# Router logits of the first batch as eight more columns of the first expert's down products

## The chip, the cores and the metric

The kernel runs on one core of one Trainium2 chip. A core has TensorE (PE, with its weight loads as PEld), VectorE (DVE), ScalarE (ACT), GpSimd (POOL), and SyncE (SP), which issues transfers. Each engine works through its own queue in order and waits on semaphores that others raise. The metric is the device time of one execution in microseconds (us), as the median of several runs.

## The reference

Two layers over x of 2 x 1024 tokens by 256. The part that matters here lies in the first layer, between attention and a mixture of experts. The input of the router is the output of an expert MLP that is picked once per batch:

```python
expert = jnp.argmax(opcode_onehot, axis=-1)
up = jnp.einsum('bsd,bhd->bsh', x, wu) + bu[:, None, :]
gate = jnp.einsum('bsd,bhd->bsh', x, wg) + bg[:, None, :]
hidden = jax.nn.silu(up) * gate
out = jnp.einsum('bsh,bdh->bsd', hidden, wd) + bd[:, None, :]
...
x = hidden_states.reshape(N, d)          # out of the MLP above
logits = x @ Wg.T                        # 8 experts
top_v, top_i = jax.lax.top_k(logits, K)  # K = 2
pos = jnp.cumsum(onehot, axis=0) - 1     # a token's place with its expert
keep = pos_f < cap                       # cap = 640
exp_batches = jnp.zeros((E, cap, d), x.dtype).at[flat_e, pos_safe].set(x[tok], mode='drop')
```

Eight experts with GELU work on these batches, and their outputs are added with the gates. Attention stands ahead of this; a second layer (three MLPs, a scan, adapters and a feed-forward part) stands behind it.

## The kernel before

All products are fp32 values split in a high and a low part, and three products stand for one: high by high, low by high, high by low (`products`, L1093, whose three matmuls are L1095 to L1097). The 2048 tokens are four chunks of 512, `c` = 0 to 3; chunks 0 and 1 are batch 0, chunks 2 and 3 batch 1. A chunk has four tiles of 128 tokens.

The order on every engine is written out by hand in `plan()`: it appends units to one list per engine, and each program below walks its list. A unit waits by `ready(...)` for the units that it reads, and a unit on PE also for the one that held its PSUM bank before. The banks go round in rings: `work` has banks 0 to 2, `down` 3 to 5, `turn2` bank 6.

For chunk c, `up_units` puts eight units on PE: `up(c, i, part)` for i = 0 to 3, each six products of 128x512. For each i, ACT takes `silu` and `hid_hi` (L1494, L1500) and DVE `prod0` and `hid_lo` (L1789, L1793). `down(c, t)` is one tile of 128 tokens by 256 features, twelve products, and DVE's `xrow` (L1802) adds the bias of the down weights and so frees the bank; SP writes the rows to memory, from where they are gathered later by expert. The down bias comes by two small gathers that POOL issues in `phase0` (L2131) behind that of the second batch's expert weights (L2129).

The logits don't use the rows. `wg(b)` forms the router's weights through the down weights (512 by 8) once per batch, `lgT(c)` multiplies the hidden values with their high and low parts as 16 stationary columns (L1223, L1224, eight products of 128x512), ACT's `lg_row` copies the result, and `lg(c)` adds the two parts and turns them (L1230). DVE then finds the largest (`first`) and the second (`second`, `m16`, `first_row`), PE counts (`cnt`), DVE works out places (`pos`, `place`, `digits`) and `at` (L1858 to L1860), from which PE's `inv` (L1247) sums up the list of tokens by slot. Its last one releases the gathers.

The first expert's weights of batch 1 are split in six pieces, ACT's `w0_hi` (L1485) and POOL's `w0_lo_pool` (L2140). Every `up` of chunks 2 and 3 waits for the last of POOL's pieces:

```python
pe.wait_ge(*ready("x1_lo", c))
pe.wait_ge(*ready("w0_lo_pool" if b else "w0_lo", b, PIECES0 - 1))
```

These pieces come from a second generator, `weights`, which is moved one step at each `yield` of `all_chunks`; where a yield stands in `all_chunks` therefore sets where a piece stands on ACT and POOL.

## Time and profile before

| what | value |
|---|---|
| median of 3 runs | 940.58 us (940.43 to 941.33) |
| profiled execution | 934.67 us |
| its span, first to last instruction | 933.4 us |
| instructions | 13194 |
| PE busy | 919.2 us, 98% |
| DVE busy | 530.1 us, 57% |
| ACT busy | 446.8 us, 48% |
| POOL busy | 269.1 us, 29% |
| granted TensorE clock, mean | 1.000 |
| of the chain that ended last, on PE | 88% |

All rows are of this one profiled execution. Matmuls are pipelined, so the length shown for one (0.39 us for 128x512) is longer than the distance from its start to the next one's start; a price on PE is read from starts. On the other engines the length of one and the start of the next tell what it costs its queue. A row's bracket tells how long the engine was idle ahead of it and who ended that. The mean of a group mixes what stands in it.

### The profile page before, as it was taken

The page shows a single profiled execution, that of the slowest core. Times are in us where ns is not written, and L with a number is a line of the kernel's source. Part 1 is how long each engine was busy: PE and PEld are TensorE (multiplying, and loading weights), DVE is VectorE, ACT ScalarE, POOL GpSimd, SP SyncE. Part 2 cuts the span into 40 slices and gives each one's busy share as a digit, 9 for nine tenths or more (in the row PEclk, how much of TensorE's full clock was granted, in tenths as well). Part 3 has the DMA queues.
Part 4 walks back from the last instruction along what each step waited for, and adds up shares of the span by engine and source line. Part 5 has one row for each costly group of instructions (what it writes and reads, how often), then busy time and mean ns, then how long its engine had stood idle before and what let it go on. Part 6 is the DMA issues. An engine that isn't in the chain of part 4 may idle for free.

```text
span 933.4 us, 13194 instructions
## 1 busy us (share of the span) xinstructions
PE 919.2 (98%) x4895; PEld 773.6 (83%) x4895; DVE 530.1 (57%) x972; ACT 446.8 (48%) x831; POOL 269.1 (29%) x243
## 2 busy tenths in 40 slices
PE   7999999999999999999999999999999999999998
PEld 4768878888799999998888888888888888888786
DVE  6754453586757766786565564334333335688544
ACT  3666565433355545674343353353342443345775
POOL 1533221220275765664410153042140230010000
PEclk9999999999999999999999999999999999999999
DMA  8030001202255443432503003003003012000011
GB/s 299 30 113 23 25 1 68 80 23 96 67 142 148 144 154 135 126 107 86 180 23 136 23 23 136 1 0 136 1 1 136 0 44 92 1 1 1 0 46 46
DMA packets 22193, 67.49 MB, mean 72 GB/s; under 512 B 4514, under 2 KB 11954, under 8 KB 19314
## 3 DMA queue, kind: packets, MB, share of 16 engines
q1 hardware_dynamic: 16546, 40.15, 11.8%
q0 software_dynamic: 5440, 26.50, 9.6%
q8 instruction: 40, 0.66, 0.3%
q14 instruction: 23, 0.19, 0.1%
q10 hardware_dynamic: 144, 0.00, 0.0%
HBM read 55.09 MB, written 9.45 MB: 69 GB/s over the span
## 4 chain that ended last, share of the span: by engine, by line
PE 88%; DVE 5%; ACT 2%; issue 2%; DMA 2%; POOL 1%; SPq 0%; ACTq 0%; DVEq 0%; POOLq 0%
PE banks L1095 19%; PE banks L1097 18%; PE banks L1096 18%; PE banks L1328 5%; PE banks L1330 5%; PE banks L1329 5%; PE banks L1187 3%; PE banks L1171 2%; PE banks L1380 2%; PE banks L1379 2%; PE banks L1178 1%; PE banks L1367 1%; PE banks L1366 1%; DMA weight_stage<-in_cond_w 1%; PE banks L1255 1%
## 5 line engine op out<-in xcount | busy, mean ns | idle before, releaser
L1095 PE MATMUL banks<-input_hi,mlp_hi 128*128 128x512 f32 x376 | 147.6, 392 | 0.0
L1097 PE MATMUL banks<-input_hi,mlp_lo 128*128 128x512 f32 x376 | 146.4, 389 | 0.0
L1096 PE MATMUL banks<-input_lo,mlp_hi 128*128 128x512 f32 x376 | 146.4, 389 | 0.0
L1590 ACT CAST hidden_hi<-hidden 128x512 fp32r<-128x512 f32 x96 | 59.6, 621 | 161.2 <-DVE hidden L1995 110.0
L2185 POOL TENSOR_TENSOR mlp_lo<-weight_stage,mlp_hi 128x768 fp32r<-128x768 f32 x32 | 59.0, 1845 | 172.4 <-ACT mlp_hi L1564 172.4
L2001 DVE TENSOR_TENSOR hidden_lo<-hidden,hidden_hi 128x512 fp32r<-128x512 f32 x96 | 66.4, 692 | 62.0 <-ACT hidden_hi L1590 61.6
L1995 DVE SCALAR_TENSOR_TENSOR hidden<-banks,L_expert_weight,gelu 128x512 f32<-128x512 f32 x64 | 48.0, 751 | 84.8 <-PE banks L1097 81.3
L1584 ACT ACTIVATE gelu<-banks 128x512 f32<-128x512 f32 x96 | 57.4, 598 | 63.8 <-PE banks L1097 63.6
L1097 PEld LDWEIGHTS banks<-input_hi,mlp_lo 128*128 128x128 f32 x376 | 70.6, 188 | 14.8
L1095 PEld LDWEIGHTS banks<-input_hi,mlp_hi 128*128 128x128 f32 x376 | 70.6, 188 | 14.3
L1096 PEld LDWEIGHTS banks<-input_lo,mlp_hi 128*128 128x128 f32 x376 | 70.6, 188 | 14.3
L1095 PE MATMUL banks<-expert_in_hi,ffn_w_hi 128*128 128x256 f32 (+1 forms) x256 | 80.0, 313 | 0.1
L1097 PE MATMUL banks<-expert_in_hi,ffn_w_lo 128*128 128x256 f32 (+1 forms) x256 | 78.8, 308 | 0.0
L1096 PE MATMUL banks<-expert_in_lo,ffn_w_hi 128*128 128x256 f32 (+1 forms) x256 | 78.8, 308 | 0.0
L1328 PE MATMUL banks<-hidden_hi,mlp_hi 128*128 128x512 f32 x192 | 75.1, 391 | 0.0
L1330 PE MATMUL banks<-hidden_hi,mlp_lo 128*128 128x512 f32 x192 | 74.8, 390 | 0.0
L1329 PE MATMUL banks<-hidden_lo,mlp_hi 128*128 128x512 f32 x192 | 74.7, 389 | 0.0
L2145 POOL TENSOR_TENSOR ffn_w_lo<-weight_stage,ffn_w_hi 128x512 fp32r<-128x512 f32 x42 | 54.4, 1297 | 32.8 <-ACT ffn_w_hi L1523 32.7
L1927 DVE TENSOR_TENSOR expert_hidden_lo<-hidden,expert_hidden_hi 128x256 fp32r<-128x256 f32 (+1 forms) x64 | 46.4, 725 | 25.9 <-ACT expert_hidden_hi L1542 25.2
L2157 POOL DMA_INDIRECT gathered<-routed_input,token_of_slot x40 | 39.4, 984 | 72.2 <-DMA routed_input<-x_rows 56.0
L1997 DVE TENSOR_TENSOR hidden<-banks,gelu 128x512 f32<-128x512 f32 x32 | 22.1, 691 | 48.4 <-PE banks L1097 48.0
L1095 PEld LDWEIGHTS banks<-expert_in_hi,ffn_w_hi 128*128 128x128 f32 x256 | 48.4, 189 | 0.8 <-issue 0.6
(333 smaller groups left out, 2169.0 us busy)
## 6 DMA issues: line engine op xcount, KB each, us to landing
weight_stage<-in_packF SPq DMA_DIRECT2D x8, 1536.0 KB, 7.6
weight_stage<-in_shared SPq DMA_DIRECT2D x2, 3072.0 KB, 10.1
expert_output<-y_rows SPq DMA_DIRECT2D x40, 128.0 KB, 2.3
weight_stage<-in_cond_w SPq DMA_DIRECT2D x4, 512.0 KB, 5.4
residual<-in_xT SPq DMA_DIRECT2D x4, 512.0 KB, 11.1
first_half_swapped<-first_half SPq DMA_DIRECT2D x16, 128.0 KB, 2.1
routed_input<-x_rows SPq DMA_DIRECT2D x16, 128.0 KB, 1.7
weight_stage<-in_ffn_w SPq DMA_DIRECT2D x2, 1024.0 KB, 8.8
```

The source lines that it names most:

```text
L1095: pe.matmul(o, wh, dh, start=(i == 0), stop=False)
L1096: pe.matmul(o, wh, dl, start=False, stop=False)
L1097: last = pe.matmul(o, wl, dh, start=False, stop=(i == len(terms) - 1))
L1328: pe.matmul(o, dh[:, i, ms], hiD[r][:, :], start=first, stop=False)
L1329: pe.matmul(o, dh[:, i, ms], loD[r][:, :], start=False, stop=False)
L1330: last = pe.matmul(o, dl[:, i, ms], hiD[r][:, :], start=False, stop=final)
L1584: act.activation(gelu_t[n % 2][:, :], bank(("gu", *key, 0)), ACT.Gelu_apprx_tanh, bias=0.0).then_inc(done)
L1590: act.copy(hiD[n % 4][:, :], prod_t[n % 2][:, :]).then_inc(done)
L1995: dve.scalar_tensor_tensor(prod_t[m % 2][:, :], o, wsel[:, n // 3, n % 3:n % 3 + 1], gelu_t[m % 2][:, :], ALU.mult, ALU.mult).then_inc(done)
L2001: dve.tensor_tensor(loD[m % 4][:, :], prod_t[m % 2][:, :], f(hiD[m % 4][:, :]), ALU.subtract).then_inc(done)
L2145: pool.tensor_tensor(lo, src, f(hi), ALU.subtract).then_inc(done)
L2185: pool.tensor_tensor(wDl[s][:, qs], stage[:, qs], f((wDh if n else wDl)[s][:, qs]), ALU.subtract).then_inc(done)
```

## The change

For batch 0 the router's weights through the down weights (high and low part) are written beside the down weights, as eight columns more. A down tile of chunks 0 and 1 is then 264 columns wide, and its last eight are the logits. `lgT`, `lg_row` and `lg` of chunks 0 and 1 are gone. The bias of the logits is a row of eight values now, copied once behind the down bias, and `xrow` adds both. Batch 1 keeps the old way.

The order changes too. The down tiles of chunk 0 and 1 stand in the middle of the next chunk's up units, behind i = 1, each followed by its `xrow` on DVE; the routing follows them; `inverse(0)` stands behind the first down tile of chunk 1. `x_rows` is one tile of eight rows' places, where six tiles were.

```diff
@@ -49,6 +49,8 @@
+DW = D + 64
+DL = D + G
@@ -382,61 +384,46 @@
 
     def all_chunks():
         yield from ups
-        yield from up_units(1, 0, 2)
-        logits(0)
-        yield
-        yield from up_units(1, 2, 3)
-        product("turn2", "lg", 0)
-        dve.append(("first", 0))
-        yield from up_units(1, 3, HT)
-        two_largest(0)
-        for t in range(QT - 1):
-            down(0, t)
-            yield
-        rows_of(0, 0, 1, 2)
-        logits(1)
-        yield
-        down(0, 3)
-        rows_of(0, 3)
-        product("down", "cnt", 0)
-        places(0)
-        yield
-        product("turn2", "lg", 1)
-        dve.append(("digits", 0))
-        dve.append(("first", 1))
-        for c in range(2, NCH):
-            between = routed_behind_first(c - 1)
-            yield from up_units(c, 0, 2, between)
+        for c in range(1, CPB + 1):
+            yield from up_units(c, 0, 2)
             if c == 2:
                 dve.append(("at", 0))
-            yield from up_units(c, 2, HT, between)
-            if c == NCH - 1:
-                use("down", [(3,), (4,), (5,), (0,), (1,), (2,)])
-            for t in range(QT - 2):
+            for t in range(QT):
                 down(c - 1, t)
+                rows_of(c - 1, t)
                 if c == 2 and t == 0:
                     inverse(0)
                 yield
-            rows_of(c - 1, 0)
-            dve.append(("at", c - 1))
-            if c < NCH - 1:
-                down(c - 1, 2)
-                yield
-            logits(c)
+            dve.append(("first", c - 1))
+            between = routed_behind_first(c - 1)
+            yield from up_units(c, 2, HT, between)
+            yield from between
+        last = NCH - 1
+        yield from up_units(last, 0, 1)
+        dve.append(("at", last - 2))
+        logits(last - 1)
+        yield
+        yield from up_units(last, 1, 2)
+        product("turn2", "lg", last - 1)
+        dve.append(("first", last - 1))
+        between = routed_behind_first(last - 1)
+        yield from up_units(last, 2, HT, between)
+        yield from between
+        inverse(last - 2)
+        use("down", [(3,), (4,), (5,), (0,), (1,), (2,)])
+        for t in range(QT - 2):
+            down(last - 1, t)
             yield
-            rows_of(c - 1, 1, 2)
-            if c == NCH - 1:
-                down(c - 1, 2)
-                yield
-            else:
-                down(c - 1, 3)
-                rows_of(c - 1, 3)
-            product("turn2", "lg", c)
-            dve.append(("first", c))
-            if c < NCH - 1:
-                inverse(c - 1)
-            yield
-        last = NCH - 1
+        rows_of(last - 1, 0)
+        dve.append(("at", last - 1))
+        logits(last)
+        yield
+        rows_of(last - 1, 1, 2)
+        down(last - 1, 2)
+        yield
+        product("turn2", "lg", last)
+        dve.append(("first", last))
+        yield
         two_largest(last)
         down(last - 1, 3)
         rows_of(last - 1, 3)
...
-    xrow = [sb("x_rows", [P, D]) for _ in range(6)]
+    xrow = sb("x_rows", [P, 2 * QT, DL])
...
+    def with_router(ap):
+        return ap[:, 2 * KD * H0:2 * KD * H0 + HT * DW].rearrange("p (k n) -> p k n", n=DW)
...
             elif kind == "down":
                 c, t = key
                 b, n, ts = c // CPB, c % 2, slice(t * P, (t + 1) * P)
-                dh, dl = parts(wBh[b], H0)[2], parts(wBl[b], H0)[2]
+                width = D if b else DL
+                dh, dl = (parts(w[b], H0)[2] if b else with_router(w[b])[:, :, 0:DL] for w in (wBh, wBl))
+                if not b:
+                    pe.wait_ge(*ready("wg_lo", b))
                 pe.wait_ge(*ready("hid_lo", c, HT - 1))
-                products(o[:, 0:D], [(hidH[n][:, k, ts], hidL[n][:, k, ts], dh[:, k, :], dl[:, k, :]) for k in range(HT)], done)
+                products(o[:, 0:width], [(hidH[n][:, k, ts], hidL[n][:, k, ts], dh[:, k, :], dl[:, k, :]) for k in range(HT)], done)
...
-                    last = pe.matmul(o[0:G, HT * G:HT * G + 1], wgT[:, m, :], by_row[b][:, KD * H0 + m:KD * H0 + m + 1], start=(m == 0), stop=(m == KD - 1))
+                    bias = by_row[b][:, KD * H0 + m:KD * H0 + m + 1]
+                    if b:
+                        last = pe.matmul(o[0:G, HT * G:HT * G + 1], wgT[:, m, :], bias, start=(m == 0), stop=(m == KD - 1))
+                    else:
+                        last = pe.matmul(o[:, HT * G:(HT + 1) * G], bias.broadcast_to((P, P)), wgT[:, m, :], start=(m == 0), stop=(m == KD - 1))
...
-                act.copy(lgb[b][0:G, :], bank(("wg", b))[0:G, HT * G:HT * G + 1])
-                act.copy(wg16[b][:, :, 0:G], bank(("wg", b))[:, 0:HT * G].rearrange("p (k g) -> p k g", g=G)).then_inc(done)
+                if b:
+                    act.copy(lgb[0:G, :], bank(("wg", b))[0:G, HT * G:HT * G + 1])
+                else:
+                    act.copy(lgb_row[:, :], bank(("wg", b))[:, HT * G:(HT + 1) * G])
+                hi = wg16[:, :, 0:G] if b else with_router(wBh[b])[:, :, D:DL]
+                act.copy(hi, bank(("wg", b))[:, 0:HT * G].rearrange("p (k g) -> p k g", g=G)).then_inc(done)
...
-                dve.tensor_tensor(wg16[b][:, :, G:2 * G], bank(("wg", b))[:, 0:HT * G].rearrange("p (k g) -> p k g", g=G), f(wg16[b][:, :, 0:G]), ALU.subtract).then_inc(done)
+                hi, lo = (wg16[:, :, 0:G], wg16[:, :, G:2 * G]) if b else (with_router(w[b])[:, :, D:DL] for w in (wBh, wBl))
+                dve.tensor_tensor(lo, bank(("wg", b))[:, 0:HT * G].rearrange("p (k g) -> p k g", g=G), f(hi), ALU.subtract).then_inc(done)
...
         def token_logits(c):
+            if c < CPB:
+                return xrow[:, c % 2 * QT:(c % 2 + 1) * QT, D:DL]
             return bank(("lg", c))[:, 0:QT * G].rearrange("p (t g) -> p t g", g=G)
...
             elif kind == "xrow":
                 c, t = key
-                n = c * QT + t
-                if n >= 6:
-                    dve.wait_ge(st_x[n % 6], 16 * (n // 6))
+                n, width = c * QT + t, DL if c < CPB else D
+                if n >= 2 * QT:
+                    dve.wait_ge(st_x[n % (2 * QT) // 2], 32 * (n // (2 * QT)))
                 if t == 0:
                     dve.wait_ge(ld["bdown"], 16 * B)
                 dve.wait_ge(*ready("down", c, t))
-                dve.tensor_tensor(xrow[n % 6][:, :], bank(("down", c, t))[:, 0:D], downB[c // CPB][:, :], ALU.add).then_inc(done)
+                if n == 0:
+                    step(dve.tensor_copy(downB[0][:, D:DL], lgb_row[:, :]))
+                dve.tensor_tensor(xrow[:, n % (2 * QT), 0:width], bank(("down", c, t))[:, 0:width], downB[c // CPB][:, 0:width], ALU.add).then_inc(done)
             elif kind == "wg_lo":
...
-                dve.wait_ge(*ready("lg", c))
+                dve.wait_ge(*(ready("xrow", c, QT - 1) if c < CPB else ready("lg", c)))
...
-            sp.dma_start(rows_in[1 + tt * P:1 + (tt + 1) * P, :], xrow[tt % 6][:, :]).then_inc(st_x[tt % 6], 16)
+            sp.dma_start(rows_in[1 + tt * P:1 + (tt + 1) * P, :], xrow[:, tt % (2 * QT), 0:D]).then_inc(st_x[tt % (2 * QT) // 2], 16)
```

Three places, each of before and then of the change. First PE, behind the second pair of up units of chunk 1 (`router_through_down` holds the router's weights through the down weights, `expert_hi` and `expert_lo` the first expert's weights):

```order
L1096 MATMUL banks<-input_lo_53,expert_hi_121 128x512
L1097 MATMUL banks<-input_hi_52,expert_lo_122 128x512
L1223 MATMUL banks<-hidden_hi_133,router_through_down_77 16x512
L1224 MATMUL banks<-hidden_lo_134,router_through_down_77 16x512
L1223 MATMUL banks<-hidden_hi_133,router_through_down_77 16x512
L1224 MATMUL banks<-hidden_lo_134,router_through_down_77 16x512
```

```order
L1098 MATMUL banks<-input_lo_53,expert_hi_120 128x512
L1099 MATMUL banks<-input_hi_52,expert_lo_121 128x512
L1097 MATMUL banks<-expert_hi_120,hidden_hi_132 128x264
L1098 MATMUL banks<-expert_lo_121,hidden_hi_132 128x264
L1099 MATMUL banks<-expert_hi_120,hidden_lo_133 128x264
L1097 MATMUL banks<-expert_hi_120,hidden_hi_132 128x264
```

The 16-wide logit products are gone from here, and the down tiles of chunk 0, 264 columns wide, stand in their place.

DVE at `at(0)` (`at_low` to `token_at_column`), behind the second hidden tile of chunk 2 (`hidden_lo`):

```order
L1793 TENSOR_TENSOR hidden_lo_134<-hidden_132,hidden_hi_133 128x512
L1858 TENSOR_TENSOR at_low_164<-ramp_low_159,column_and_low_157 128x1024
L1859 TENSOR_TENSOR column_hit_161<-ramp_158,column_and_low_157 128x320
L1860 TENSOR_TENSOR token_at_column_162<-column_hit_161,token_number_160 128x320
L1789 SCALAR_TENSOR_TENSOR hidden_131<-banks,expert_biases_126,silu_129 128x512
L1839 TENSOR_SCALAR row_154<-place_82 128x8
```

```order
L1804 TENSOR_TENSOR hidden_lo_133<-hidden_131,hidden_hi_132 128x512
L1872 TENSOR_TENSOR at_low_158<-ramp_low_153,column_and_low_151 128x1024
L1873 TENSOR_TENSOR column_hit_155<-ramp_152,column_and_low_151 128x320
L1874 TENSOR_TENSOR token_at_column_156<-column_hit_155,token_number_154 128x320
L1815 TENSOR_TENSOR x_rows_136<-banks,expert_bias_down_126 128x264 x4
L1674 TENSOR_REDUCE two_largest_80<-x_rows_136 128x4
```

`at(0)` kept its place behind that tile; the four rows of chunk 1 and their largest logit now follow it at once, where the third hidden tile and the routing's digits stood.

ACT, the high pieces of the second expert's weights (`expert_hi<-weight_stage`) among the hidden tiles of chunk 1:

```order
L1500 CAST hidden_hi_135<-hidden_132 128x512
L1512 ACTIVATE logit_parts_143<-banks,logit_bias_79 16x512
L1494 ACTIVATE silu_129<-banks,expert_biases_123 128x512
L1500 CAST hidden_hi_135<-hidden_131 128x512
L1485 CAST expert_hi_124<-weight_stage_54 128x512 x2
L1494 ACTIVATE silu_130<-banks,expert_biases_123 128x512
L1500 CAST hidden_hi_135<-hidden_132 128x512
L1485 CAST expert_hi_124<-weight_stage_54 128x512 x4
L1488 COPY expert_biases_126<-weight_stage_54 128x8
```

```order
L1508 CAST hidden_hi_134<-hidden_131 128x512
L1493 CAST expert_hi_123<-weight_stage_54 128x512 x3
L1502 ACTIVATE silu_128<-banks,expert_biases_122 128x512
L1508 CAST hidden_hi_134<-hidden_130 128x512
L1493 CAST expert_hi_123<-weight_stage_54 128x512 x2
L1502 ACTIVATE silu_129<-banks,expert_biases_122 128x512
L1508 CAST hidden_hi_134<-hidden_131 128x512
L1493 CAST expert_hi_123<-weight_stage_54 128x512
L1496 COPY expert_biases_125<-weight_stage_54 128x8
```

Two pieces stood behind chunk 1's third hidden tile and four behind its fourth; now three stand behind the second, two behind the third, and the last alone behind the fourth.

## Rows read from the trace of the kernel before

**Rows 1.** The page, busy time of each engine, us (share of the span) xinstructions.

```profile
PE 919.2 (98%) x4895; PEld 773.6 (83%) x4895; DVE 530.1 (57%) x972; ACT 446.8 (48%) x831; POOL 269.1 (29%) x243
```

**Rows 2.** Timeline of PE, chunk 1; columns: start us, length us, engine, line, operation.

```profile
175.85 0.39 PE L1223 MATMUL banks<-hidden_hi,router_through_down 128*16 128x512 f32 x1
...
177.70 0.39 PE L1095 MATMUL banks<-input_hi,expert_hi 128*128 128x512 f32 x1
...
180.53 1.05 PE L1230 MATMUL banks<-sum_of_parts,logit_parts 16*128 16x8 f32 x8
181.51 0.50 PE L1095 MATMUL banks<-input_hi,expert_hi 128*128 128x512 f32 x1
```

**Rows 3.** Timeline of PE, from the second router product on.

```profile
188.60 1.85 PE L1214 MATMUL banks<-router_weights,down_by_row 128*128 128x8 f32 x16
190.38 0.24 PE L1216 MATMUL banks<-down_by_row,router_weights 128*8 128x1 f32 x4
190.56 0.41 PE L1223 MATMUL banks<-hidden_hi,router_through_down 128*16 128x512 f32 x1
...
193.14 0.39 PE L1095 MATMUL banks<-expert_hi,hidden_hi 128*128 128x256 f32 x1 [0.54 <-DVE x_rows L1802]
...
194.67 0.18 PE L1239 MATMUL banks<-routed_bf,earlier_token 128*128 128x8 bf16 x1
...
195.10 1.05 PE L1230 MATMUL banks<-sum_of_parts,logit_parts 16*128 16x8 f32 x8
```

**Rows 4.** Timeline of PE, a down tile of chunk 1 and the inverse.

```profile
207.55 0.28 PE L1095 MATMUL banks<-expert_hi,hidden_hi 128*128 128x256 f32 x1
...
208.97 0.96 PE L1247 MATMUL banks<-token_at_column,at_low 128*128 128x40 f32 x8
```

**Rows 5.** Groups of PE's instructions by form; busy us, mean ns of one.

```profile
L1095 PE MATMUL banks<-expert_in_hi,ffn_w_hi 128*128 128x384 f32 x128 | 43.7, 341 | 0.0
```

**Rows 6.** Timeline of DVE, chunk 1, the third hidden tile and the first comparisons.

```profile
180.74 0.75 DVE L1789 SCALAR_TENSOR_TENSOR hidden<-banks,expert_biases,silu 128x512 f32<-128x512 f32 x1 [2.30 <-PE banks L1097]
182.17 0.69 DVE L1793 TENSOR_TENSOR hidden_lo<-hidden,hidden_hi 128x512 fp32r<-128x512 f32 x1 [0.69 <-ACT hidden_hi L1500]
182.78 0.18 DVE L1664 TENSOR_REDUCE two_largest<-banks 128x4 f32<-128x32 f32 x1
183.00 0.19 DVE L1665 TENSOR_TENSOR route_tmp<-banks,two_largest 128x32 f32<-128x32 f32 x1
183.22 0.86 DVE L1666 TENSOR_TENSOR route_tmp<-route_tmp,eight_minus_expert 128x32 f32<-128x32 f32 x1
```

**Rows 7.** Timeline of DVE, chunk 2, the routing of chunk 1 and at(0).

```profile
199.25 0.75 DVE L1789 SCALAR_TENSOR_TENSOR hidden<-banks,expert_biases,silu 128x512 f32<-128x512 f32 x1 [0.92 <-PE banks L1097]
...
201.55 0.69 DVE L1793 TENSOR_TENSOR hidden_lo<-hidden,hidden_hi 128x512 fp32r<-128x512 f32 x1
...
204.37 1.22 DVE L1858 TENSOR_TENSOR at_low<-ramp_low,column_and_low 128x1024 fp32r<-128x1024 f32 x1
...
206.02 0.49 DVE L1860 TENSOR_TENSOR token_at_column<-column_hit,token_number 128x320 fp32r<-128x320 f32 x1
```

**Rows 8.** Timeline of ACT, last hidden tile of chunk 1 and the weights.

```profile
186.17 0.62 ACT L1500 CAST hidden_hi<-hidden 128x512 fp32r<-128x512 f32 x1 [2.27 <-DVE hidden L1789]
186.70 2.18 ACT L1485 CAST expert_hi<-weight_stage 128x512 fp32r<-128x512 f32 x4
```

**Rows 9.** Timeline of POOL, gathers and low parts of the second expert.

```profile
175.40 0.95 POOL L2131 DMA_INDIRECT expert_bias_down<-in_b_down,expert_of_L_cond  x1 [0.30 <-issue]
...
187.39 5.01 POOL L2140 TENSOR_TENSOR expert_lo<-weight_stage,expert_hi 128x512 fp32r<-128x512 f32 x4 [2.09 <-ACT expert_hi L1485]
```

**Rows 10.** The down bias's tile: its two gathers from issue to landing.

```profile
DMA to landing us min/median/max: 4.9/5.3/5.7
```

**Rows 11.** Timeline of PE, filler products at the program's start and at 245.78.

```profile
3.81 6.13 PE L1121 MATMUL banks<-earlier_token,identity_bf 128*128 128x512 bf16 x18 [3.81 <-POOL partition_number L2096]
...
245.78 5.35 PE L1121 MATMUL banks<-earlier_token,identity_bf 128*128 128x512 bf16 x24
```

More of the change, by code:

```diff
@@ L881, in program @@
     both_parts = sb("sum_of_parts", [2 * G, G])
-    wg16 = [sb("router_through_down", [P, HT, 2 * G], F32R) for _ in range(B)]
-    lgb = [sb("logit_bias", [2 * G, 1]) for _ in range(B)]
+    wg16 = sb("router_through_down", [P, HT, 2 * G], F32R)
+    lgb = sb("logit_bias", [2 * G, 1])
+    lgb_row = sb("logit_bias_by_row", [P, G])
     all_top2, all_places, all_first_rows, raw_gates, kept = (sb(n, [P, NCH, K, QT]) for n in
@@ L928, in program @@
             assert top[0] <= projected_top
-    downB = [sb("expert0_bias_down", [P, D]) for _ in range(B)]
+    downB = [sb("expert0_bias_down", [P, D if b else DW]) for b in range(B)]
     silu_t = [sb("silu", [P, CH]) for _ in range(2)]
@@ L938, in program @@
             assert top[0] <= scored_top
-    xrow = [sb("x_rows", [P, D]) for _ in range(6)]
-    lg16 = [sb("logit_parts", [2 * G, CH]) for _ in range(2)]
+    xrow = sb("x_rows", [P, 2 * QT, DL])
+    lg16 = [sb("logit_parts", [2 * G, CH]) for _ in range(NCH - CPB)]
     lg2, pos = (sb(n, [P, QT, G]) for n in ("logits_but_first", "position"))
@@ L1041, in program @@
     ld = {n: nc.alloc_semaphore(f"ld_{n}") for n in names}
-    st_x = [nc.alloc_semaphore(f"st_x{i}") for i in range(6)]
+    st_x = [nc.alloc_semaphore(f"st_x{i}") for i in range(QT)]
     st_y = [nc.alloc_semaphore(f"st_y{i}") for i in range(4)]
@@ L1045, in program @@
     constants = nc.alloc_semaphore("constants")
-    CONSTS = 10
+    CONSTS = 9
     pool_parts = nc.alloc_semaphore("pool_parts")
@@ L1065, in program, with pieces0, from_stage0 @@
     rope_no = {u: n for n, u in enumerate(rope_units)}
+    def pieces0(ap, b):
+        if b:
+            return [ap[:, q * W0N // PIECES0:(q + 1) * W0N // PIECES0] for q in range(PIECES0)]
+        ups = [ap[:, q * H0:(q + 1) * H0] for q in range(2 * KD)]
+        downs = ap[:, 2 * KD * H0:2 * KD * H0 + HT * DW].rearrange("p (k n) -> p k n", n=DW)
+        return ups + [downs[:, k:k + 2, 0:D] for k in range(0, HT, 2)]
+    def from_stage0(b, q):
+        ap = stage[:, b * PK0 + q * W0N // PIECES0:b * PK0 + (q + 1) * W0N // PIECES0]
+        return ap if b or q < 2 * KD else ap.rearrange("p (k n) -> p k n", n=D)
+    def with_router(ap):
+        return ap[:, 2 * KD * H0:2 * KD * H0 + HT * DW].rearrange("p (k n) -> p k n", n=DW)
     def qt_of(c, i):
@@ L1222, in tensor_program @@
                 for k in range(HT):
[L1223 to L1224 removed]
+                    pe.matmul(o[0:2 * G, :], wg16[:, k, :], hidH[c % 2][:, k, :], start=(k == 0), stop=False)
+                    last = pe.matmul(o[0:2 * G, :], wg16[:, k, :], hidL[c % 2][:, k, :], start=False, stop=(k == HT - 1))
                 last.then_inc(done)
@@ L1484, in scalar_program @@
                         act.wait_ge(*ready(*last))
-                act.copy(wBh[b][:, qs], stage[:, b * PK0:(b + 1) * PK0][:, qs]).then_inc(done)
+                act.copy(pieces0(wBh[b], b)[q], from_stage0(b, q)).then_inc(done)
             elif kind == "b0":
@@ L1504, in scalar_program @@
                 act.wait_ge(*ready("wg", b))
-                act.copy(lgb[b][0:G, :], bank(("wg", b))[0:G, HT * G:HT * G + 1])
-                act.copy(wg16[b][:, :, 0:G], bank(("wg", b))[:, 0:HT * G].rearrange("p (k g) -> p k g", g=G)).then_inc(done)
+                if b:
+                    act.copy(lgb[0:G, :], bank(("wg", b))[0:G, HT * G:HT * G + 1])
[3 more added lines that the diff above has]
+                act.copy(hi, bank(("wg", b))[:, 0:HT * G].rearrange("p (k g) -> p k g", g=G)).then_inc(done)
             elif kind == "lg_row":
                 c, = key
-                if c >= 2:
-                    act.wait_ge(*ready("lg", c - 2))
                 act.wait_ge(*ready("lgT", c))
-                act.activation(lg16[c % 2][:, :], bank(("lgT", c))[0:2 * G, :], ACT.Identity, bias=lgb[c // CPB][:, 0:1]).then_inc(done)
+                act.activation(lg16[c % 2][:, :], bank(("lgT", c))[0:2 * G, :], ACT.Identity, bias=lgb[:, 0:1]).then_inc(done)
             elif kind == "wf_hi":
@@ L2152, in pool_program @@
                     pool.wait_ge(ld["small"], SMALL)
-                    for i in range(6):
-                        pool.wait_ge(st_x[i], 16 * len(range(i, NT, 6)))
+                    for i in range(QT):
+                        pool.wait_ge(st_x[i], 16 * (NT // QT))
                 if n > ST:
```

19 lines of the change are left out of this document (7 added, 12 removed).

## The prediction

> **What bounds the kernel now.** I read the page first. TensorE (PE) is busy for 919.2 of 933.4 us [rows 1], and the chain that ended last lies on PE for nearly all of its length. So a change is worth what it takes from PE's queue, less every new wait of PE. The change touches one stretch, from the first up products of chunk 1 (about 170 us) to the inverse of the routing (246 us). There I read the timeline of each engine. PE runs without a gap but for one wait, in front of the fourth down tile of chunk 0, at 193.14 [rows 3]. The reader is to look at start-to-start distances in that view, since the shown lengths overlap. Behind 246 us nothing is changed, so a shift of this stretch should reach the end unchanged.
>
> Prices from start to start: an up unit (six 128x512 products) 1.39 us, a down tile (twelve 128x256) 207.55 to 208.97 = 1.42 us [rows 4]. The first is six eighths of the eight 128x512 products that took 1.85 us from 175.85 [rows 2]. Below, E is the time at which PE goes on to its next unit behind the up unit in question.
>
> **What goes.** Per chunk of the first batch, the eight 16-wide products of the logits through the down weights (175.85 to 177.70 = 1.85 us) and the sum of their parts (180.53 to 181.51 = 0.98 us) [rows 2]; the first up product behind the latter is some 0.1 us slower than usual, and that goes too. Two chunks: 2 x (1.85 + 0.98 + 0.1) = 5.9 us. The old wait for a bank goes as well: the logit products from 190.56 end at 190.56 + 1.85 = 192.4, and the tile starts at 193.14, 0.7 us later; it took 194.67 - 193.14 = 1.53 instead of 1.42 us, so 0.8 us together [rows 3]. Sum of gains: 6.7 us. ScalarE's two copies of the logits go too, beside PE's work, worth nothing by themselves.
>
> **What is added on PE.** Eight tiles of twelve products get eight columns more. From 128x512 (1.85 / 8 = 0.231 us) and 128x256 (1.42 / 12 = 0.118 us) a column costs 0.44 ns, so 96 x 8 x 0.44 ns = 0.34 us. The first batch's bias of the logits is now two fp32 products that fill 128 rows and 8 columns; four bias instructions took 190.56 - 190.38 = 0.18 us, and sixteen 8-column ones 190.38 - 188.60 = 1.78 us, 0.11 each [rows 3]; 4 x 0.11 - 0.18 = 0.26 us. Sum: 0.6 us. The copy of the bias into VectorE's (DVE's) row is 0.2 us, counted below.
>
> **New wait 1, fourth down tile of chunk 0: 0.9 us (0 to 1.7).** The down tiles of chunk 0 move ahead of the third pair of up units, to 175.85. Three tiles of 1.46 us end at 180.2, and the fourth needs the first tile's bank, which DVE frees by adding the down bias. That bias comes by GpSimd's (POOL's) second small gather, issued at 175.40 [rows 9] and landing 4.9 us later [rows 10], at 180.3. Before, it was first wanted for the tile that started at 193.14 [rows 3]. Copy 0.2, add 0.42 and a signal give 181.0, so 0.8 us, and 0.1 us for the slow restart [rows 3]. If the gathers land earlier it is nothing; with 5.7 us instead of 4.9 us, 1.7.
>
> **New wait 2, first up unit of chunk 2: 2.6 us (1.3 to 3.9).** This unit needs the last low piece of the second expert's weights from POOL. Before, ScalarE (ACT) did the last four high pieces in a row behind hid_hi(1,3), from 186.70, and POOL had the low ones ready at 187.39 + 5.01 = 192.40, while PE came to the unit behind 195.10 only [rows 3, 8, 9]. Now only the last piece stands there, but hid_hi(1,3) waits for prod0(1,3), and on DVE this stands behind hid_lo(1,2) and the routing of chunk 0. From E of up(1,2,1): prod0(1,2) at 0.21 (180.53 to 180.74) [rows 2, 6], then second largest and masks until hid_lo(1,2) is due at 0.21 + 2.30 = 2.51 (199.25 to 201.55 is 2.30) [rows 7]. Meanwhile ACT has hid_hi(1,2) at 0.99 (0.21, 0.75 for prod0, 0.03) and the next piece at 1.52, and POOL starts 0.69 later, at 2.21 (186.17, 186.70, 187.39) [rows 8, 9]. A POOL piece lasts 1.25 us (5.01 for four) [rows 9].
>
> The row of 183.22 shows a comparison of 32 elements, both inputs in SBUF, that took 0.86 us and ended with POOL's piece, while its neighbour at 183.00, reading PSUM, took 0.19 under the same piece [rows 6]. I take the same wait for hid_lo(1,2): it starts at 2.21 + 1.25 = 3.46, then prod0(1,3) at 4.07 (0.61 on, as 182.17 to 182.78 [rows 6]), hid_hi(1,3) at 4.85 (0.78), the last high piece at 5.38 (0.53), and POOL could start at 6.07 (0.69), but hid_lo(1,3), by then due behind the places, holds it until about 6.36. End 7.61. PE is there after two up units, the counts (194.67 to 195.10) and the router product (188.60 to 190.56) [rows 3], at 2.78 + 0.43 + 1.96 = 5.17. Wait 2.5 us and 0.1 for the restart. With no clash at all the chain ends at 6.4 (1.3 us); with one piece more in the way it is 3.9.
>
> The Trainium skill, page "SBUF — State Buffer", section "Who interferes with whom", says that a DVE instruction with two SBUF inputs and a GpSimd instruction that reads SBUF exclude each other for the whole instruction. The trace agrees on the small comparisons; that the 0.69 us hid_lo is held in the same way no row of this stage shows. By the rule the wait is 2.6 us, without it 1.3. It also speaks against the change in that the comparisons of chunk 0's logits now read SBUF where they read PSUM.
>
> **New wait 3, inverse(0) behind the first down tile of chunk 1: 3.1 us (2.9 to 3.3).** The inverse needs at(0), three wide DVE instructions, and DVE has these behind hid_lo(2,1). From E of up(2,1,1) the chain prod0, hid_hi, hid_lo ends, by the rows of chunk 1, at 182.78 - 180.53 = 2.25 [rows 2, 6]. at(0) takes 204.37 to 206.51 = 2.14 [rows 7], a signal 0.05: 4.44. PE has only one down tile (1.46) to do there, where it had four up units and the counts more before. 4.44 - 1.46 = 3.0, and 0.1 for the restart. Nothing in this chain depends on how late PE came, so earlier gains don't shorten it. At 208.97 in the old order inverse(0) had no wait [rows 4].
>
> **Moved without price.** The rows of x go out earlier by SP's queue and have eight buffers instead of six; the gather needs only the last ones. The fetch of the next packed weights moves ahead of its old place on SP, with nothing behind it that is late. In chunk 3 the 16-wide products stand two up units behind their chunk, ACT and DVE have them by then. The tail from down(2,0) on has the old order on PE; DVE has digits(2) 1.2 us later, before a place where it waited for PE.
>
> **The sum.** Gains 6.7; costs 0.6 + 0.9 + 2.6 + 3.1 = 7.2; 0.5 us slower. The profiled run took 934.67 us with a span of 933.4, so its like would be 935.2; the runs shown have a median of 940.58, 5.9 above it, and 941.1 is the forecast. Its own range, with the ends of waits 1 and 2, is 938.9 to 943.2; its upper end is the second rival.
>
> **Rivals.**
> - Clock falls (slower). TensorE stands still for 3.0 us at wait 3 and 2.5 us at wait 2. At the program's start, after 3.8 us of nothing, 18 filler products took 6.13 us, where 24 took 5.35 us behind a busy stretch (0.223 each) [rows 11]; 18 of those would be 4.0, so the start at the 1.2 GHz level cost 2.1 us. If a wait throws the clock from 2.4 to 1.2 GHz, it costs 2.1 us a time: 943.2, or 945.3 for both. It decides from an idle time between 0.7 us, which left the products behind it at the old pace [rows 3], and 3.8 us. Against it: both waits are shorter than 3.8.
> - More clashes with POOL (slower). Waits 1 and 2 at their upper ends: 941.1 + 0.8 + 1.3 = 943.2.
> - Wide products are dearer (slower). If 264 columns cost as much as 384 (0.34 us as shown against 0.28 [rows 5, 4]), that is 96 x 0.06 = 5.8 instead of 0.34: 946.6.
> - The waits don't come (faster). If bias and weights are early enough, waits 1 and 2 vanish and only wait 3 stays: 6.7 - 0.6 - 3.1 = 3.0 faster, 937.6. For it: before, POOL ended at 192.40 and was not needed until 195.1 [rows 3, 9]. Against it: the order of ACT.
>
> **How the numbers follow.** A measurement of this kernel can tell 0.2% (1.9 us) from no change. The forecast has 0.65, nearly all of it within 0.2%; the clock 0.13 (a third of it for both waits); more clashes 0.09; dear columns 0.03; no waits 0.10. So faster 0.10, same 0.65, slower 0.25. The range 938.7 to 943.3 leaves out the last two and the two-fold clock loss, 0.17 in all.
>
> **What would show it.** In the trace after: no 16-wide logit products before chunk 2; 128x264 products 3 to 4 ns apart from the old pace; PE idle before the fourth down tile of chunk 0 (released by x_rows) of 0.8 us, before the first up product of chunk 2 (released by POOL's expert_lo) of 2.5, and before the first inverse (released by DVE's token_at_column) of 3.0; the inverse of the last chunk gives way to the 24 fillers at 245.78 + 0.5 [rows 11]. I am wrong if the last two are below 1 us, or if products behind them run at half pace, or if the fillers start more than 2 us off.

## The result, and the profile after

The changed kernel takes 946.65 us (median of five runs, 944.91 to 947.43), the kernel before 940.43 beside it: a ratio of 1.0068, with a 95% interval of 1.0055 to 1.0081. It is 6.2 us slower, where 0.5 us was forecast, and it lies outside the range. The profiled run took 946.62 us with a span of 945.4.

The page after, busy time of each engine, which answers to [rows 1]:

```profile
PE 920.3 (97%) x4863; PEld 775.4 (82%) x4863; DVE 526.8 (56%) x973; ACT 445.3 (47%) x829; POOL 270.4 (29%) x242
```

The waits of PE by line (us in total, times, longest):

```profile
PE banks L1123 <- POOL partition_number L2110: 3.8, 1, 3.8
PE banks L1097 <- POOL expert_lo L2153: 3.7, 1, 3.7
PE banks L1256 <- DVE token_at_column L1874: 3.1, 1, 3.1
PE banks L1097 <- ACT gelu L1546: 1.8, 1, 1.8
...
PE banks L1097 <- DVE x_rows L1815: 0.4, 1, 0.4
```

PE has 32 products fewer and yet is busy for 1.1 us more. So beside the new waits something made the work itself slower. The timeline of PE at the places of the three waits and at the fillers:

```profile
176.74 0.28 PE L1097 MATMUL banks<-expert_hi,hidden_hi 128*128 128x264 f32 x1
...
190.99 0.24 PE L1223 MATMUL banks<-down_by_row,router_weights 128*8 128x1 f32 x4
194.92 0.76 PE L1097 MATMUL banks<-input_hi,expert_hi 128*128 128x512 f32 x1 [3.69 <-POOL expert_lo L2153]
...
202.29 0.28 PE L1097 MATMUL banks<-expert_hi,hidden_hi 128*128 128x264 f32 x1
...
206.98 0.48 PE L1256 MATMUL banks<-token_at_column,at_low 128*128 128x40 f32 x3 [3.05 <-DVE token_at_column L1874]
...
213.85 0.39 PE L1097 MATMUL banks<-input_hi,expert_hi 128*128 128x512 f32 x1
...
251.41 0.82 PE L1123 MATMUL banks<-earlier_token,identity_bf 128*128 128x512 bf16 x3
```

The fillers start at 251.41, 5.63 us later than in [rows 11]. Four up units take 202.29 - 194.92 = 7.37 us, where four of 1.39 are 5.56. The inverse and three down tiles take 213.85 - 206.98 = 6.87, where the run with fillers below needs 209.93 - 204.58 = 5.35. The view by windows gives the reason (columns: window, its length; busy us and instructions of PE, weight load, DVE, ACT, POOL; granted clock; DMA share; GB/s):

```profile
186.00:191.00 5.00, 5.00 (x44) 4.29 (x44) 4.42 (x10) 2.25 (x4) 2.56 (x2) 1.00 0.02 3
191.00:195.00 4.00, 0.31 (x6) 0.24 (x5) 3.83 (x10) 1.36 (x5) 1.42 (x1) 0.62 0.00 0
195.00:198.00 3.00, 3.00 (x7) 2.37 (x8) 0.59 (x5) 0.14 (x1) 0.00 (x0) 0.50 0.00 0
199.00:202.00 3.00, 3.00 (x15) 2.47 (x14) 1.40 (x2) 1.21 (x2) 0.00 (x0) 1.00 0.00 0
204.00:207.00 3.00, 0.02 (x1) 0.05 (x1) 2.88 (x5) 0.05 (x1) 0.00 (x0) 1.00 0.00 0
...
210.00:212.00 2.00, 2.00 (x11) 2.00 (x11) 0.37 (x1) 0.00 (x0) 0.00 (x0) 0.50 0.20 67
214.00:216.00 2.00, 2.00 (x11) 1.60 (x10) 1.39 (x6) 0.56 (x1) 0.00 (x0) 1.00 0.49 136
```

Behind each of the two long standstills there is a stretch at the 1.2 GHz level (0.50): from 192.0 to 198.8, and from 209.0 to 212.5. While PE works in them it does half the products in the same time. This costs 7.37 - 5.56 = 1.8 and 6.87 - 5.35 = 1.5 us. The trace of before has 1.00 in the whole stretch. The trace after has one more stretch at 0.50, from 270.5 to 273.9, behind the fillers and the wait of 1.8 us for ScalarE's gelu.

### The profile page after: what moved, and what is told of

Read it like the earlier page. It is cut to its first block, busy times and chain, and to the rows that moved or that the text cites. A ratio compares the mean times of both kernels' runs of the same rounds, so it can differ in the third digit from the quotient of the medians.

```text
span 945.4 us, 13120 instructions
## 1 busy us (share of the span) xinstructions
PE 920.3 (97%) x4863; PEld 775.4 (82%) x4863; DVE 526.8 (56%) x973; ACT 445.3 (47%) x829; POOL 270.4 (29%) x242
## 4 chain that ended last, share of the span: by engine, by line
PE 86%; DVE 5%; issue 3%; ACT 2%; DMA 2%; POOL 1%; SPq 0%; ACTq 0%; DVEq 0%; POOLq 0%
PE banks L1097 18%; PE banks L1099 18%; PE banks L1098 18%; PE banks L1337 5%; PE banks L1339 5%; PE banks L1338 5%; PE banks L1189 3%; PE banks L1173 2%; PE banks L1389 2%; PE banks L1388 2%; PE banks L1180 1%; PE banks L1376 1%; PE banks L1375 1%; DMA weight_stage<-in_cond_w 1%; PE banks L1264 1%
## 5 line engine op out<-in xcount | busy, mean ns | idle before, releaser
L1099 PE MATMUL banks<-input_hi,mlp_lo 128*128 128x512 f32 x376 | 146.5, 389 | 0.0
L1941 DVE TENSOR_TENSOR expert_hidden_lo<-hidden,expert_hidden_hi 128x256 fp32r<-128x256 f32 (+1 forms) x64 | 44.5, 696 | 26.2 <-ACT expert_hidden_hi L1552 24.8
L1099 PEld LDWEIGHTS banks<-expert_in_hi,ffn_w_lo 128*128 128x128 f32 x256 | 48.6, 190 | 0.5 <-issue 0.5
```

The lines of the kernel that those rows point to most:

```text
L1099: last = pe.matmul(o, wl, dh, start=False, stop=(i == len(terms) - 1))
```

## The experiments

The runs were made on more than one chip, and the kernel before took 935.2, 939.8 and 940.5 us in three comparisons. So each kernel is held against the kernel before of its own comparison, and what is compared across them is the difference.

**The two kernels again.** Unchanged, for more traces.

> The kernel before, unchanged, for a second trace. The trace of it that the prediction used came from a run of 934.7 us with a granted clock of 1.000, while its median is 940.4. First theory: an ordinary run of it shows a time near 940, has the clock at half level in one or two stretches of 3 to 4 us (1.6 to 2 us each) behind waits of TensorE in the expert stage, and needs about 6 us more than the old trace behind 250 us; up to the 24 fillers (245.8) it stays within 1 us of the old trace. Rival: the 6 us are spread evenly over the span, or lie in the stretch that the change touches, so that the change's own cost is nearer 12 us than 6.

It took 934.7 us at a clock of 1.000, and before had a median of 935.19 in its comparison, so this tells only that the old trace is a faithful one where before takes 935. The run near 940 that the expectation wanted to look at was not caught, and its question stayed open here.

> The changed kernel, unchanged, beside the kernels of this call, so that all differences are of one chip. Expected 6 us (0.6 to 0.7%) above the kernel before, with TensorE's waits of 3.7 us (first up product of chunk 2) and 3.1 us (inverse of chunk 0) and half clock behind both, and the 24 fillers at about 251, 5.6 us later than before. If the loss of 6 us belongs to the chip of the first comparison and not to the kernel, it is 0 to 3 us here.

945.6 us against 939.79: ratio 1.0064 (1.0048 to 1.0080), 5.8 us slower. The waits are the same to 0.1 us. The half clock cost more here, 8.40 instead of 5.56 us for the four up units and 8.36 instead of 5.35 for inverse and tiles, and the fillers start at 253.23. What follows is shorter, 944.4 - 253.23 = 691.2 us against 945.4 - 251.41 = 694.0: the clock stays at 1.00 behind the fillers, where it fell once in the first trace.

> The kernel before, unchanged, once more. Medians of it were 940.4, 935.2 and 939.8 in three comparisons, on more than one chip; both traces of it are of 934.7. If this run is one near 940, its trace should show where the 5 us lie: expected behind 250 us, in the first products of the first routed expert, where the changed kernel's traces near 940 show a wait of 1.7 us for ScalarE's gelu that its traces near 935 don't, and at the start. Rival: they lie in the stretch of the change.

938.29 us, of the kind wanted. Its timeline of PE, at the fillers and at a product of the first routed expert:

```profile
245.99 0.39 PE L1121 MATMUL banks<-earlier_token,identity_bf 128*128 128x512 bf16 x1
...
264.05 0.41 PE L1095 MATMUL banks<-expert_in_hi,ffn_w_hi 128*128 128x384 f32 x1 [1.91 <-issue]
```

The fillers start at 245.99, 0.2 us off the old trace; the span left behind them is 937.0 - 245.99 = 691.0 us, against 933.4 - 245.78 = 687.6 in the old trace. So the difference between these two traces lies behind the stretch of the change, 1.9 us of it in one wait in front of the wide products of the first routed expert, and it is no part of what the change costs.

**The inverse later.** Only this line differs from the changed kernel:

```
-                if c == 2 and t == 0:
+                if c == 2 and t == QT - 1:
                     inverse(0)
```

> The changed kernel with one edit: the inverse of chunk 0 stands behind the fourth down tile of chunk 1 and not behind the first. This takes away the wait of 3.1 us for DVE's token_at_column. First theory (a wait costs its length and, behind it, a stretch at half clock): 3.1 + 1.6 = 4.7 us faster than the changed kernel, about 942.0. Rival (the clock fall is not tied to this wait, or would come anyway): 3.1 us, 943.6. Second rival (the wait is hidden or turns up elsewhere): no change, 946.6.

935.97 us against 935.19, ratio 1.0009 (0.9999 to 1.0019). That is 0.8 us above before, where the changed kernel stood 5.8 to 6.2 above: the edit is worth 5.0 to 5.4 us. The wait itself was 3.1, and the stretch at half clock behind it is gone. The first theory gave 4.7, its rival 3.1. The changed kernel itself was not run on this chip, so the gain takes its loss to be the same here as in the two comparisons that have it. The other wait stayed, 3.7 us, with half clock behind it (24 up products in 202.41 - 194.15 = 8.26 us):

```profile
194.15 0.77 PE L1097 MATMUL banks<-input_hi,expert_hi 128*128 128x512 f32 x1 [3.68 <-POOL expert_lo L2153]
...
202.41 0.28 PE L1097 MATMUL banks<-expert_hi,hidden_hi 128*128 128x264 f32 x1
```

**Fillers in the waits.** The changed kernel with

```
+            if c == 2:
+                spin(16, 1)
             yield from up_units(c, 0, 2)
...
                 if c == 2 and t == 0:
+                    spin(13, 7)
                     inverse(0)
```

> The changed kernel with TensorE kept busy in the two long waits by filler products whose result nobody reads: 16 (3.6 us) in front of the first up product of chunk 2, and 13 (2.9 us) in front of the inverse of chunk 0. The waits on DVE and GpSimd stay as long as they are. First theory (the idle time is followed by a fall of the clock that costs by itself): 1.8 + 1.6 = 3.4 us faster than the changed kernel, 943.2, with the granted clock at 1.00 from 190 to 214 us. Rival (the clock fall has another cause, or costs nothing): 946.6 as the changed kernel.

937.39 us against 935.19, ratio 1.0027 (1.0016 to 1.0037): 2.2 us above before, so 3.6 to 4.0 less than the changed kernel, though PE goes on at the same point behind the first wait, 18.1 us behind its first down tile (18.2 in the changed kernel). The windows, and PE's timeline at the first filler, the first up product behind the wait and the down tile behind the up products:

```profile
191.00:194.00 3.00, 3.00 (x16) 1.26 (x13) 2.86 (x8) 1.36 (x5) 1.14 (x1) 1.00 0.00 0
195.00:198.00 3.00, 3.00 (x15) 2.46 (x14) 0.62 (x2) 0.69 (x1) 0.00 (x0) 1.00 0.00 0
...
210.00:212.00 2.00, 2.00 (x10) 1.62 (x10) 1.38 (x6) 0.48 (x1) 0.00 (x0) 1.00 0.37 128
```

```profile
190.67 0.39 PE L1126 MATMUL banks<-earlier_token,identity_bf 128*128 128x512 bf16 x1
...
194.41 0.47 PE L1100 MATMUL banks<-input_hi,expert_hi 128*128 128x512 f32 x1
...
199.97 0.28 PE L1100 MATMUL banks<-expert_hi,hidden_hi 128*128 128x264 f32 x1
```

From 194.41 to 199.97 are 5.56 us, the full pace. From 195 to 198 us, where the changed kernel did 7 products, 15 are done. Work that nobody needs, put into a wait, bought back the loss of the clock: 3.4 us were expected. This is the run that separates the clock from the idle time.

**Half of the wait filled**, beside all of it, both on top of the later inverse (so with one wait, of 3.7 us).

> The changed kernel with the inverse of chunk 0 behind the fourth down tile of chunk 1, and 16 filler products in the wait in front of the first up product of chunk 2. The wait's length stays. The kernel with the later inverse alone stood 0.8 us above before, and its 24 up products behind the wait took 8.26 us where 5.56 is the full pace. First theory: these 2.7 us go, 1.9 us (0.2%) below the kernel before. Rival: 0.8 above it, as without fillers.

> As the kernel with the later inverse and 16 fillers, but with 8, so that TensorE works for 1.8 us of the wait and then stands still for 1.9. If a standstill of 1.9 us is enough for the clock to fall (behind one of 1.8 us at 267 us the changed kernel shows half clock), the time is that of no fillers, 0.8 us above the kernel before. If it isn't, it is that of 16 fillers, 1.9 below it.

939.46 and 939.89 us against 939.79; ratios 0.9991 (0.9980 to 1.0002) and 0.9993 (0.9983 to 1.0002). The medians don't tell the two apart, nor either from before, and the 1.9 us below before that were expected with 16 fillers are not in them. The traces do tell them apart: with 16 fillers the up products behind the wait take 5.53 us (194.71 to 200.24) at a clock of 1.00, 2.7 us less than without fillers, as expected; with 8 they take 7.16, behind a standstill of 1.86 us (windows of the kernel with 8):

```profile
192.00:194.00 2.00, 0.36 (x2) 0.00 (x0) 1.96 (x4) 0.81 (x5) 1.34 (x1) 1.00 0.00 0
195.00:196.00 1.00, 1.00 (x5) 0.76 (x4) 0.00 (x0) 0.00 (x0) 0.00 (x0) 0.67 0.00 0
196.00:198.00 2.00, 2.00 (x6) 1.62 (x5) 0.00 (x0) 0.69 (x1) 0.00 (x0) 0.50 0.00 0
```

So 1.86 us of standstill can be enough, at least with the small products shortly before it. It doesn't seem to happen every time: the mean clock of the whole span was 0.996 in six of that kernel's eleven runs and 0.999 or 1.000 in the other five, while with 16 fillers it was never below 0.998.

**The weights earlier.** All six high pieces of the second expert's weights in front of silu(1,2), the main lines of the edit:

```
-            if q < PIECES0 - 1:
+            if q < PIECES0 - 1 and not b:
                 yield
...
-    weights = chain([None] * 6, split0(1), ...
+    weights = chain([None] * 8, split0(1), ...
```

> The changed kernel with one edit: ScalarE's six high pieces of the second expert's weights stand together in the gap in front of silu(1,2) (where it had three), so that GpSimd is done with the low ones at about 189 instead of 194.8 us. First theory: the wait of 3.7 us in front of the first up product of chunk 2 goes, and the half clock behind it (1.8): 5.5 us faster than the changed kernel, 941.1. Rival (the clock has nothing to do with the wait): 3.7 us, 942.9. Second rival: six pieces in a row on GpSimd hold up more small DVE operations, so the down tiles and products beside it get later by 1 to 2 us: 942 to 943.5 with the clock at its full level.

938.59 us against 935.19, ratio 1.0033 (1.0022 to 1.0044): 3.4 above before, only 2.4 to 2.8 gained. The wait for expert_lo is gone, but POOL now works from 180.50 to 188.05 without a pause, and DVE's routing of chunk 0 runs beside it. DVE's timeline, PE's, and the windows:

```profile
184.38 1.22 DVE L1678 TENSOR_TENSOR route_tmp<-route_tmp,eight_minus_expert 128x32 f32<-128x32 f32 x1
...
185.86 1.00 DVE L1680 TENSOR_TENSOR expert_onehots<-eight_minus_expert,eight_minus_picked 128x32 f32<-128x32 f32 x1
```

```profile
189.59 0.17 PE L1250 MATMUL banks<-routed_bf,earlier_token 128*128 128x8 bf16 x1 [1.25 <-DVE routed_bf L1834]
```

```profile
191.00:195.00 4.00, 4.00 (x18) 3.58 (x19) 2.34 (x12) 0.89 (x4) 0.00 (x0) 0.50 0.00 0
195.00:197.00 2.00, 2.00 (x6) 1.60 (x5) 0.00 (x0) 0.69 (x1) 0.00 (x0) 0.50 0.00 0
```

The counts came 1.25 us late, which is the second rival, and the clock fell all the same, between 190 and 191: the standstill was short, but the 20 small products of the router followed at once. They took 3.2 us instead of 2.0, and the up products 7.51 instead of 5.56. So the first theory was wrong to tie the fall to the long wait alone. The wait of 3.1 us for the inverse stayed, with half clock behind it.

**One held-up operation less.** The changed kernel with DVE's first_row moved behind the places:

```
         dve.append(("m16", c))
-        dve.append(("first_row", c))
...
         dve.append(("place", c))
+        dve.append(("first_row", c))
```

> The changed kernel with one edit: DVE's first_row, the small comparison between the masks and hid_lo(1,2) that took 1.25 us beside GpSimd's piece where 0.16 is its time alone, stands behind the places. First theory (the wait of 3.7 us is the predicted 2.5 plus one more held-up operation): hid_lo(1,2) is done 1.1 us earlier or more, GpSimd's last piece as well, and the wait is 2.5 us; with half clock behind it as before, 1.2 us faster than the changed kernel, 5 us (0.5%) above the kernel before. Rival: hid_lo, as a wide instruction, waits for both pieces anyway: 3.7 us as before and no gain, 6 us above.

945.1 us against 940.48, ratio 1.0050 (1.0036 to 1.0064), 4.6 us above before. This interval overlaps with those of the changed kernel, so the reading rests on the traces. DVE's timeline and POOL's row in the changed kernel:

```profile
188.45 1.25 DVE L1835 TENSOR_SCALAR first_row<-eight_minus_picked 128x8 f32<-128x8 f32 x1
189.74 1.71 DVE L1804 TENSOR_TENSOR hidden_lo<-hidden,hidden_hi 128x512 fp32r<-128x512 f32 x1
191.37 0.74 DVE L1800 SCALAR_TENSOR_TENSOR hidden<-banks,expert_biases,silu 128x512 f32<-128x512 f32 x1
```

```profile
188.34 2.56 POOL L2153 TENSOR_TENSOR expert_lo<-weight_stage,expert_hi 128x512 fp32r<-128x512 f32 x2 [3.50 <-ACT expert_hi L1493]
```

The same in this kernel, and its wait of PE for the weights:

```profile
188.27 1.78 DVE L1804 TENSOR_TENSOR hidden_lo<-hidden,hidden_hi 128x512 fp32r<-128x512 f32 x1
189.97 0.74 DVE L1800 SCALAR_TENSOR_TENSOR hidden<-banks,expert_biases,silu 128x512 f32<-128x512 f32 x1
...
191.55 0.17 DVE L1835 TENSOR_SCALAR first_row<-eight_minus_picked 128x8 f32<-128x8 f32 x1
```

```profile
PE banks L1097 <- POOL expert_lo L2153: 2.7, 1, 2.7
```

In the changed kernel POOL has two pieces in a row, from 188.34 to 190.90. The tiny first_row, a multiply and add on 8 values a partition, was held up beside the first of them (1.25 us; 0.17 where POOL is idle), the wide hid_lo beside the second (1.71 us; 0.69 alone). With first_row out of the way hid_lo is held up by one piece only, and the wait is 2.7 us, 1.0 less. This is the predicted case of one clash, at the predicted size.

**Two versions that beat both.** The later inverse, and the pieces as four in front of silu(1,2) and two behind hid_hi(1,2):

```
-            if q < PIECES0 - 1:
-                yield
+            yield from [None] * ((1, 1, 0, 1, 0, 2)[q] if b else int(q < PIECES0 - 1))
```

> The changed kernel with the inverse of chunk 0 behind the fourth down tile of chunk 1, and ScalarE's six high pieces of the second expert's weights as four in front of silu(1,2) and two behind hid_hi(1,2) (three, two and one in the changed kernel). GpSimd should end at about 190.8 and TensorE come at 190.2, so that the wait of 3.7 us shrinks to about 0.6. First theory: 3.1 us of wait and the 2.7 us that the half clock cost behind it in the kernel with the later inverse go: 5.8 us less than that kernel, so about 5 us (0.5%) below the kernel before. Rival: the clock falls even so, since the 20 small products of the router in front stay, and TensorE loses 2 to 3 us: 2 to 3 us below before. Second rival: DVE's small operations held up by GpSimd make the counts wait 1.2 us, as they did with six pieces in a row: 4 us below before.

936.29 us against 939.79, ratio 0.9959 (0.9946 to 0.9972), 3.5 us below before: between the expected 5 and the rival. PE doesn't wait for the weights, and yet the windows show:

```profile
183.00:188.00 5.00, 5.00 (x24) 4.13 (x23) 4.43 (x12) 1.53 (x3) 2.85 (x3) 1.00 0.21 66
189.00:191.00 2.00, 2.00 (x28) 1.98 (x25) 1.97 (x2) 0.41 (x1) 1.93 (x2) 1.00 0.00 0
...
192.00:195.00 3.00, 3.00 (x8) 2.34 (x7) 2.48 (x13) 1.53 (x5) 0.00 (x0) 0.50 0.00 0
```

PE is busy throughout, but from 188.7 to 191.1 with small products alone (the counts and the router's), and the clock fell between 191 and 192; the four up units took 7.21 us. The last kernel adds two edits to this one: it moves the router's products away from the counts, and it lets each group of up products wait only for the pieces that it reads. The main lines:

```
         act.append(("b0", b))
+        if b:
+            yield from [None] * 3
         product("out", "wg", b)
...
-                pe.wait_ge(*ready("w0_lo_pool" if b else "w0_lo", b, PIECES0 - 1))
+                pe.wait_ge(*ready("w0_lo_pool" if b else "w0_lo", b, 2 * part + 1 if b else PIECES0 - 1))
...
```

> The kernel with four and two pieces and the later inverse (3.5 us below before), with the 20 small products of the second batch's router moved from in front of chunk 2 to behind its first three up products' groups, and the wait of each group of up products cut to the pieces of weights that it reads. In the kernel without this the clock fell at 191.9 us with TensorE busy, behind these small products, and cost 1.6 us. First theory (the counts and the router's products, 2.4 us of small products in a row, let the clock fall; apart from each other they don't): the clock stays, 1.6 us less, 5 us (0.55%) below the kernel before. Rival: the 2 us of small products alone are enough: the fall only moves to about 194, no gain. Second rival: ScalarE comes too late with silu(2,0) and TensorE waits 1 to 2 us in front of the second unit: 3 us below before.

934.76 us against 940.48, ratio 0.9938 (0.9925 to 0.9952), **5.7 us below before**. PE's timeline at the router's products and at the fillers, and two windows, with those products and behind them:

```profile
191.60 0.28 PE L1222 MATMUL banks<-router_weights,down_by_row 128*128 128x8 f32 x2
...
241.33 0.39 PE L1124 MATMUL banks<-earlier_token,identity_bf 128*128 128x512 bf16 x1
```

```profile
192.00:193.00 1.00, 1.00 (x11) 1.00 (x11) 0.87 (x4) 0.91 (x3) 0.00 (x0) 1.00 0.00 0
194.00:196.00 2.00, 2.00 (x11) 1.63 (x10) 1.19 (x5) 0.72 (x4) 0.00 (x0) 1.00 0.00 0
```

The stretch runs at 1.00 throughout, and the fillers start 4.45 us before those of [rows 11], 2.0 before those of the kernel with four and two (243.33). Whether keeping the small products apart is what holds the clock, or this one trace was lucky, is not settled: the mean clocks of the single runs (0.997 to 1.000 here, 0.996 to 1.000 with four and two) don't tell, since the clock also falls or not in the first routed expert, at 260 us in this very trace.

## Why the prediction was wrong, point by point

Two terms failed. The clock stood at nothing in the sum and cost 3.3 us in the profiled run. Wait 2 stood at 2.6 us and measured 3.7. The other terms held.

**What bounds the kernel** held: PE's queue and its waits account for the result. **The medians** held in part: a shift of the stretch by 5.63 us came out as 6.2 in the medians. The 5.9 us between the old trace and the old median were carried over as they were; the third trace of before shows 3.4 of such a difference behind the stretch and 0.2 in it, and no run shows the rest.

**Gains, 6.7 us:** right. The last experiment has them with the new waits all but removed. Less 0.3 us for columns, 1.3 for two waits for x_rows with their restarts and 0.2 for the counts they leave 4.9. From 176.28, its first down tile, to its fillers at 241.33 are 65.05 us, where [rows 2] and [rows 11] have 69.93 for the same stretch: 4.9 less.

**Added on PE, 0.6 us:** about 0.5, right. From the first to the last of thirty-six products in a row are 4.24 us with 264 columns (176.74 to 180.98), and 4.13 with 256 (184.36 to 188.49, before), so 96 cost 0.3 us more; single tiles gave up to 0.07 a tile, which would be 0.5 for all. The forecast was 0.34. From the first product of wg(0) to the first one behind its bias are 2.15 us (147.40 to 149.55) instead of 1.96 (146.60 to 148.56, before), so the bias costs 0.2 and not 0.26. The rival of dear columns fell: it asked for 5.8. The first down tile stood at 176.74, 0.89 us later than the old product in its place, but 0.80 of this was there at 147.40 already, in front of the first product of PE that the change touches. That point lies at 146.5 to 146.9 in three traces of before and at 146.6 to 147.4 in ten of the changed kernel and its variants; why is not known.

**Wait 1, 0.9 us (0 to 1.7):** 0.75 from start to start, by the mechanism named: the tile came 0.6 late, of which the view shows 0.44 as idle, and took 0.15 longer. The bias landed 4.7 us after its issue and not 4.9.

**Wait 2, 2.6 us (1.3 to 3.9):** 3.7, near the upper end. The failed step: hid_lo(1,2) was taken to be held by one POOL piece, with "the last high piece" behind. But ACT had two pieces ready for POOL at that place, and DVE has first_row in front of hid_lo, which was priced at nothing. Each of the two DVE operations was held by one POOL piece. The run with first_row moved measured 2.7. The Trainium skill, page "SBUF — State Buffer", section "Who interferes with whom", says that a tensor_scalar can enter a mode in which it takes the port pair that DVE shares with GpSimd, so that not only instructions with two SBUF inputs can be held up. The trace agrees: 1.25 us against 0.17 for first_row, a tensor_scalar. The prediction used only the half of the rule on two inputs.

**Wait 3, 3.1 us (2.9 to 3.3):** 3.2 from start to start, of which the view shows 3.05 as idle, and 0.1 for the restart: right. Its removal with the clock behind it gave 5.0 to 5.4 us.

**The clock, nothing in the sum:** 1.8 + 1.5 = 3.3 us in the profiled run. This was the first rival, priced at 2.1 us a time, and it had a chance of 0.13. The failed step is its "against it: both waits are shorter than 3.8". The row from which that came, the 3.8 us at the program's start [rows 11], bounded the idle time only from above: it said that 3.8 is followed by half clock, and nothing of 2.5 or 3.0. It was also a start and no fall, since PE had done nothing before. Between 0.7 and 3.8 there was no evidence, and the prediction took the absence of a row for a reason.

**The sum** of the measured terms for the profiled run: waits 0.75 + 3.75 + 3.3 with their restarts, 0.9 later start with the bias in it, 0.3 columns, 3.3 clock, less 6.7, gives 5.6, and the fillers are 5.63 us late. The rivals were treated as alternatives, though the clock and the second clash could come together, and did. At the prices of the prediction both together are 941.1 + 4.2 + 1.3 = 946.6, next to the measured 946.65, but that is luck in part: with the sizes of the profiled run, 3.3 and 1.1, it is 945.5, and no run shows where the last 1.1 us lie. A wait and the clock behind it depend on each other, so a case with both belonged among the rivals.

## What to carry to other kernels

Price a new wait of TensorE as its length plus a stretch at half clock behind it, unless a row of the trace shows that a standstill of that length leaves the clock alone. Move work between engines by what the consumer waits for: here another order of the same products, with finer waits, turned 6 us of loss into 5.7 us of gain. Where GpSimd works beside DVE, count its pieces and DVE's operations beside them one by one, the 8-element ones too.

## What was not expected of the hardware

All standstills of TensorE of 2.7 us and more within the routing stretch, eight in five traces, were followed by half clock, for 3.4 to 6.9 us, at a cost of 1.5 to 3.0. Four of them, in front of the inverse, stood behind wide products alone; the other four, in front of chunk 2, stood behind the 2.4 us of small products too, so what part these had there is not shown. Standstills of 1.7 to 1.9 us, in front of the wide products of the first routed expert, were followed by it in four of eight traces. And it fell with TensorE busy, behind 2.4 us of small products, in the one trace of the kernel with four and two.

The mean clock also goes with a part of the scatter of the kernel before. In one comparison its 23 runs are thirteen with a mean clock of 0.998 and a median of 940.79 us, nine with 1.000 and 939.30, and one with 0.999. That the 0.998 comes from a fall behind the wait in the first routed expert is a guess: none of the three traces of before has such a fall. The 5 us between the comparisons are not the clock, since the runs at 1.000 near 935 and near 939 both have it in full.
